# A gated cross-attention block with mixture of experts on one core: the shared expert rebuilt as one unit of 704 columns

## The reference

```python
x = x + tanh(g_xattn[1]) * attention(layernorm(x), ctx)        # 16 heads, the stage before
h = layernorm(x)
probs = softmax(h @ router_w.T)                                # 8 experts
topk_w, topk_idx = top_k(probs, 2); topk_w = topk_w / sum(topk_w)
moe = sum over the two chosen e of topk_w * (silu(h @ gate_w[e]) * (h @ up_w[e])) @ down_w[e]   # 352 wide
shared = (silu(h @ s_gate_w + s_gate_b) * (h @ s_up_w + s_up_b)) @ s_down_w + s_down_b          # 704 wide
x = x + tanh(g_ffn[1]) * (moe + shared)
```

## Time and profile before

| | us |
|---|---|
| median of 3 runs (1182.26 to 1189.67) | 1182.75 |
| span of the profiled execution, first to last instruction | 1146.9 |
| time of that execution around its span | not given by the page |
| TensorE busy, share of span | 1028.8, 90% |
| VectorE | 747.0, 65% |
| ScalarE | 601.8, 52% |
| GpSimd | 456.0, 40% |

### The profile page before, as it was taken

One profiled execution on the slowest core, in us unless ns is written; L12 is line 12 of the kernel. 1 busy time (PEld: TensorE's weight loads), 2 busy tenths in 40 slices (PEclk: granted clock), 3 DMA queues, 4 the chain that ended last, 5 costly groups with the idle time before them and its releaser, 6 DMA issues. The chain is left out here.

```text
span 1146.9 us, 17729 instructions
## 1 busy us (share of the span) xinstructions
PE 1028.8 (90%) x5438; PEld 475.5 (41%) x5439; DVE 747.0 (65%) x1419; ACT 601.8 (52%) x898; POOL 456.0 (40%) x483
## 2 busy tenths in 40 slices
PE   0466889999789999999999998999998899999996
PEld 0243445555423223323322324455445455555542
DVE  6988988888786776578477547745545344443347
ACT  6897999999346776467467565452211111111110
POOL 1100335544410242243134341000657788889065
PEclk9978899999979999999999999998999899999998
DMA  9322930000534234134211004201678888976588
GB/s 325 114 74 80 342 138 1 2 1 9 133 89 107 80 82 116 62 58 94 66 48 44 12 21 136 76 26 52 243 282 170 200 205 207 206 192 146 153 284 291
DMA packets 174204, 142.39 MB, mean 124 GB/s; under 512 B 121364, under 2 KB 137108, under 8 KB 173624
## 3 DMA queue, kind: packets, MB, share of 16 engines
q1 hardware_dynamic: 163560, 110.40, 34.7%
q0 software_dynamic: 8672, 29.76, 7.9%
q10 hardware_dynamic: 1904, 1.38, 0.6%
HBM read 70.93 MB, written 43.37 MB: 100 GB/s over the span
## 5 line engine op out<-in xcount | busy, mean ns | idle before, releaser
L1432 ACT ACTIVATE prob<-p_col,mask_col,any_key 128x512 f32<-128x512 f32 x256 | 186.2, 781 | 103.2 <-PE p_col L1564 102.3
L1653 DVE CUSTOM_DVE_ANT_0 ajunk<-p_row,mask_row 128x512 bf16<-128x512 f32 x256 | 166.2, 686 | 64.1 <-PE p_row L1513 62.5
L1526 PE MATMUL p_out<-prob,v 128*64 128x512 f32 x512 | 138.1, 618 | 0.1
L1332 POOL TENSOR_TENSOR o<-sum_a,rec 32x512 f32<-32x512 f32 x30 | 39.1, 1304 | 186.1 <-DMA rec<-inv_d 184.0
L1513 PE MATMUL p_row<-ks,early_place 99*128 99x512 f16 x256 | 100.5, 395 | 8.7 <-DVE top L1653 8.0
L1564 PE MATMUL p_col<-early_place,ks 101*128 101x512 f16 x256 | 97.7, 385 | 0.9 <-ACT prob L1432 0.3
L2647 DVE SCALAR_TENSOR_TENSOR shid<-s_up,ssilu 128x352 f32<-128x352 f32 x39 | 20.4, 524 | 99.0 <-PE s_up L2565 98.8
L2513 ACT ACTIVATE ssilu<-s_gate 128x352 f32<-128x352 f32 x39 | 18.1, 463 | 124.0 <-PE s_gate L2565 124.0
L2578 PE MATMUL s_down<-mw,shT 128*128 (+1 forms) x351 | 82.0, 379 | 0.0
L2565 PE MATMUL s_gate<-mw,sxT 128*128 x444 | 74.1, 318 | 6.7 <-DMA sxT<-x_slots 6.7
L2565 PE MATMUL s_up<-mw,sxT 128*128 x444 | 73.5, 316 | 0.0
(11 more groups left out here) (354 smaller groups left out, 2077.3 us busy)
## 6 DMA issues: line engine op xcount, KB each, us to landing
x_slots<-nought SPq DMA_DIRECT2D x3, 3328.0 KB, 18.4
y_slots<-y SPq DMA_DIRECT2D x39, 256.0 KB, 2.2
early_place<-in_ctx SPq DMA_DIRECT2D x8, 1024.0 KB, 6.2
early_place<-halves_d SPq DMA_DIRECT2D x45, 128.0 KB, 2.5
halves_d<-halves SPq DMA_DIRECT2D x18, 256.0 KB, 2.1
mstg<-in_L_ffn_gate_w POOLq DMA_DIRECT2D x6, 704.0 KB, 5.7
mstg<-in_L_ffn_up_w POOLq DMA_DIRECT2D x6, 704.0 KB, 6.0
x<-in_x SPq DMA_DIRECT2D x4, 1024.0 KB, 7.3
```

The source lines that it names most:

```text
L1432: nc.scalar.activation(prob[s % 4][:, c, :], p_col[c][:], ACT.Exp, bias=mask_col[:, b, k:k + 1], scale=any_key[:, b:b + 1]).then_inc(t_exp, 1)
L1526: mm = nc.tensor.matmul(p_out[pr][c * 2 * DH:(c + 1) * 2 * DH, :], v1[b % 2][:, k, g, :], prob[n % 4][:, c, :], start=(k == 0), stop=(k == ...
L1653: nc.vector.tensor_tensor_reduce(junk[:, n % 2, :], p_row[n % 2][:], mask_row[:, blk // HPG, :], 1.0, -3e38, ALU.add, ALU.max, top[blk % 2 ...
```

## The change

The shared expert is one unit of 704 columns: five chunks of 128 rows for gate, five for up, and one chunk that holds the last 64 of both (`CHUNKS` 11). The high half of the last 64 hidden rows lies on partitions 0 to 63 and the low half on 64 to 127, so a down product takes 5 x 3 + 2 = 17 passes per 128 tokens in place of 18. Columns come by DMA transpose on SyncE (`turn`), those of batch 0 in attention's last but one block (`turn_kept`). The router stands after batch 1's second pair of chunks. Down products of batch 1 follow batch 2's pairs, and those of batch 2 are put off to the tail: its hidden halves are stored to `hid_d` and read back. Ten pieces of weights replace the old ones. The held weights for the tail come in two loads, at the tenth and fourteenth pair of tiles. TensorE's pairs for batch 2 and for batch 3 from the third chunk on are unrolled one by one with slices by number. Stores of packed weights are ten in place of four. The buffers `spare`, `lines` and the joined PSUM banks only change places.

```diff
+            def turn_kept():
+
+                for t in range(TPB):
+                    sp.wait_ge(t_kl, t + 1)
+                    early.turn(sp, x0T, keep, t, t_x0)
...
+                if blk == BLOCKS - 2:
+                    turn_kept()
...
+CHUNKS = 2 * (SB - 1) + 1
+CW = CHUNKS * P
+SD0 = KB * CW
+HELD = 2
+HW = 2 * HELD * P
+RW = CW - HW
+assert SD0 + SB * D == 2 * WC and 2 * SLAST == P
+HTS = 2 * SB - 1
+S_PARTS = (("gate", 0, 1), ("up", 0, 1), ("gate", 1, 2), ("up", 1, 2), ("gate", 3, 2), ("up", 3, 2), ("both", SB - 1, 1),
+           ("down", 0, 2), ("down", 2, 2), ("down", 4, 2))
+NSP = len(S_PARTS)
+ORDER = [(u, q) for u in range(EARLY) for q in range(len(W_PARTS))]
+MORE = NSP + len(ORDER) - len(W_PARTS) * (2 + EARLY)
 LATE_B = B - 1
+HELD_B = B - 2
 
 
 def rows(m):
@@ -1848,11 +1867,17 @@
     eng.dma_start(t, src).then_inc(s_w[q % 2], 16)
...
+def down_products(hT, wd):
+
+    out = []
+    for m in range(SB - 1):
+        for hs, hm in ((0, 0), (0, 1), (1, 0)):
+            out.append((hT[hs][m], wd(hm, m, P), P))
+    return out + [(hT[0][SB - 1], wd(0, SB - 1, P), P), (hT[0][SB - 1], wd(1, SB - 1, SLAST), SLAST)]
...
+            def turn(b):
+                sp.wait_ge(m_xl, b)
+                for t in range(TPB):
+                    sp.dma_start_transpose(xT[b][:, :, :, t * P:(t + 1) * P].rearrange("p h k s -> p (h k) s"),
+                                           row_of(TPB * b + t)).then_inc(m_xT[b], 16)
+
...
-
-            def weights(u, q):
-                e = UNITS_IN[u]
-                if u < 2:
-                    c = slice(u * EI, (u + 1) * EI)
-                    src = (a["L1_ffn_s_gate_w"][:, c], a["L1_ffn_s_up_w"][:, c], a["L1_ffn_s_down_w"][c, :])
-                else:
-                    src = [a["L1_ffn_" + t][e] for t in ("gate_w", "up_w", "down_w")]
-                sp.wait_ge(m_wl, ready(u, q) - 2)
-                load_part(sp, stg, m_w, q, *src)
-
-            for u, q in ORDER:
-                weights(u, q)
-            for u in range(2):
-                kept = w[:, (SHARED + u) * 2 * WC:(SHARED + u + 1) * 2 * WC].rearrange("p (h c) -> p h c", h=2)
-                sp.wait_ge(m_wl, ready(u, NQ - 1))
-                sp.dma_start(shared_d[u, :, :, 0:MAIN], kept[:, :, 0:MAIN]).then_inc(m_saved, 16)
-                sp.dma_start(shared_d[u, 0:ELAST, :, MAIN:WC], kept[0:ELAST, :, MAIN:WC]).then_inc(m_saved, 16)
-            sp.wait_ge(m_xT, NT)
+            weights_in(sp, 2)
+            weights_in(sp, 3)
+            turn(1)
+            weights_in(sp, 4)
+            weights_in(sp, 5)
+            weights_in(sp, 6)
+            turn(2)
+            weights_in(sp, 7)
+            turn(3)
+            weights_in(sp, 8)
+            weights_in(sp, 9)
+            sp.wait_ge(m_xT[LATE_B], TURNED)
             for h in range(2):
-                sp.dma_start(late_d[h], xT[:, h, :, LATE_B * S:(LATE_B + 1) * S]).then_inc(m_saved, 16)
-            sp.wait_ge(m_turn, TPB)
+                sp.dma_start(late_d[h], xT[LATE_B][:, h]).then_inc(m_saved, 16)
+            weights_in(sp, NSP)
+            weights_in(sp, NSP + 1)
+            sp.wait_ge(m_wl, NSP)
+            held_d, rest_d, down_d = shared_d
+            gates_kept = (SB - 1 - HELD) * P
+            for h in range(2):
+                first = by_row(h)[:, :, 0:2 * (SB - 1) * P].rearrange("p k (n c) -> p k n c", n=2)[:, :, :, 0:HELD * P]
+                for n in range(2):
+                    sp.dma_start(held_d[h, :, :, n], first[:, :, n]).then_inc(m_saved, 16)
+                sp.dma_start(rest_d[h, :, :, 0:gates_kept], by_row(h)[:, :, HELD * P:(SB - 1) * P]).then_inc(m_saved, 16)
+                sp.dma_start(rest_d[h, :, :, gates_kept:], by_row(h)[:, :, (SB - 1 + HELD) * P:]).then_inc(m_saved, 16)
+                sp.dma_start(down_d[h], wide(h)[:, SD0:]).then_inc(m_saved, 16)
+            for j in range(NSP + 2, NSP + len(ORDER)):
+                weights_in(sp, j)
+            sp.wait_ge(m_hl, SB * GB)
+            for m in range(SB):
+                for h in range(2 if m < SB - 1 else 1):
+                    sp.dma_start(hid_d[:, 2 * m + h, :], hT[HELD_B % 2][h][m]).then_inc(m_saved, 16)
             sp.wait_ge(m_scat, SCATTERED)
             for n in range(2):
                 sp.dma_start_transpose(first_xT[:, n].rearrange("p h k t -> p (h k) t"), x_slots[n * P:(n + 1) * P, :]).then_inc(m_first[n], 16)
-            sp.wait_ge(m_saved, 16 * 6)
+            sp.wait_ge(m_saved, 16 * (2 + 2 * 5 + HTS))
 
         @block.gpsimd
         def _(pool):
@@ -1977,11 +2078,11 @@
                 nc.gpsimd.tensor_tensor(rstd[:], veps[:], neg_half[:], ALU.pow).then_inc(m_rstd, 1)
...
+            high_parts(0, 1, 2, 3)
             act.wait_ge(m_rwt, 1)
             nc.scalar.copy(rwT[0][:], p_rw).then_inc(m_rwh, 1)
-            turned(4)
-            turned(5)
-            high(2)
-            hidden(0, 1, lambda: high_parts(1, 2, 3))
-            for t in range(6, 10):
-                turned(t)
-            high(3)
+            high(1)
+            hidden(0, lambda: high_parts(4, 5), lambda: (high(2), high_part(6)), lambda: high_part(7), lambda: None, lambda: high(3))
             act.wait_ge(m_const, CONSTS)
-            hidden(1, 0, lambda: high_part(2, 0), lambda: high_part(2, 1))
-            for t in range(10, NT):
-                turned(t)
-            act.wait_ge(m_shift, 1)
-            nc.scalar.activation(logit[:], logit[:], ACT.Exp).then_inc(m_exp, 1)
-            hidden(1, 1, lambda: high_part(2, 2), lambda: high_part(2, 3))
-            act.wait_ge(m_xl, B - 1)
-            hidden(2, 0, lambda: high_part(3, 0), lambda: high_part(3, 1))
-            hidden(2, 1, lambda: high_part(3, 2), lambda: high_part(3, 3))
+            hidden(1, lambda: high_part(8), shifted_exp(act, nc, m_shift, m_exp, logit), lambda: high_part(9), lambda: high_part(NSP),
+                   lambda: high_part(NSP + 1))
+            hidden(2, lambda: high_part(NSP + 2), lambda: high_part(NSP + 3), lambda: high_part(NSP + 4), lambda: high_part(NSP + 5),
+                   lambda: high_parts(NSP + 6, NSP + 7))
 
         @block.tensor
         def _(pe):
...
+            def weights_ready(g, i):
+
                 if g == 0:
-                    pe.wait_ge(m_wl, ready(n, NQ - 1))
-                pe.wait_ge(m_hl, EB * (u + 1))
+                    pe.wait_ge(m_wl, (2, 4, 4, 6, 6, 7)[i])
+
+            def pair(g, i):
+                c = SB * g + i
+                q = c % 2 * S
+                weights_ready(g, i)
+                need(pe, m_hid, c - 1)
+                chunk(p_gate[:, q:q + S], lambda hs, k: chunk_of(hs, i if i < SB - 1 else CHUNKS - 1, k), g).then_inc(m_gate, 1)
...
-            turn(14, 15)
+            for i in range(SB):
+                pair(0, i)
+            pe.wait_ge(m_xT[1], TURNED)
+            pair(1, 0)
+            pair(1, 1)
             router()
-            gate_up(1, 1)
-            down(1, 0)
+            pair(1, 2)
+            pair(1, 3)
+            pair(1, 4)
             number_slots()
-            gate_up(2, 0)
-            down(1, 1)
-            gate_up(2, 1)
-            down(2, 0)
-            down(2, 1)
+            pair(1, 5)
+            down(0)
+            looped_pairs(2)
+            pair(2, 5)
+            down(1)
...
+            link(nc.vector.tensor_scalar(bias[:, 1, :], bias[:, 1, :], W_UP, None, ALU.mult))
+            statistics(1)
+            low_parts(0, 1)
+            normalise(1)
+            low_parts(2, 3)
+            ready_router()
+            low_rows(1)
+            hidden(0, lambda: (low_parts(4, 5), statistics(2)), lambda: normalise(2), lambda: (low_rows(2), low_part(6)),
+                   lambda: (statistics(3), low_part(7)), lambda: normalise(3))
             low_rows(3)
-            hidden(1, 0, lambda: low_part(2, 0), lambda: low_part(2, 1))
-            add(0, 1)
-            choose()
-            hidden(1, 1, lambda: low_part(2, 2), lambda: low_part(2, 3))
-            add(1, 0)
-            find_slots()
-            hidden(2, 0, lambda: low_part(3, 0), lambda: low_part(3, 1))
-            add(1, 1)
-            hidden(2, 1, lambda: low_part(3, 2), lambda: low_part(3, 3))
-            add(2, 0)
-            add(2, 1)
-
-
-def stage_tiles(nc, sb, ps, sem, st, a, x, keep, x_slots, y_slots, out_d, w, stg, dest, share, expert_of, m_wh, m_wl,
-                bias, bias_dg, gate_dn, shared_d, late_d, m_first, first_xT):
+            hidden(1, lambda: low_part(8), weigh, lambda: (choose(), low_part(9)), lambda: shares(), find_slots)
+            find_owners()
+            down_bias()
...
-            sp.dma_start(late_w[0][:, :, U0:D0], shared_d[0, :, :, U0:D0]).then_inc(e_lu, 16)
-            sp.dma_start(late_w[1][:, :, G0:D0], shared_d[1, :, :, G0:D0]).then_inc(e_lv, 16)
-            for n, done in enumerate((e_ld0, e_ld1)):
-                sp.dma_start(late_w[n][:, :, D0:MAIN], shared_d[n, :, :, D0:MAIN]).then_inc(done, 16)
```

(82 more changed lines are left out.)

616 lines of the change are left out of this document (336 added, 280 removed).

## The result

The changed kernel takes **1202.0 us** (median of 4 runs, 1197.7 to 1206.6), the kernel before beside it 1182.9; the ratio is 1.0132, 95% interval 1.0077 to 1.0186. Forecast were 1181.5 us and at most 1195. Three further comparisons of the two (e2, e9, e14) gave 1.0112, 1.013 and 1.0071 (intervals within 1.004 to 1.021). So the change costs 9 to 19 us by the medians, where I had it at a gain of 1.4.

The account below looks back on a forecast made before the run. TensorE was taken to bound the kernel nearly everywhere. The terms +2.2 - 4.0 - 5.5 + 5.9 gave -1.4 us on a span of 1146.9, plus 35.9 carried over: 1181.5 us, no change, range 1162 to 1195.

Parts of the forecast that it names:

- attention's end: Before the shared stage: four transposes on SyncE delay the chain of sums and reciprocals, so the stage starts 2.2 us later.
- shared stage: Shared expert's stage: about 32 us less TensorE work, mostly lost to waits in batch 0's feeding chain, leaving -4.0 us.
- tile loop: Loop over tiles: moving held-weight loads later shortens one slow transpose of a tile's columns, -5.5 us.
- tail: After the tiles: 52 more products, partly hidden, make TensorE end after the last gather, +5.9 us, bounds 3 and 9.
- no load of a tile's columns over 7 us: Sign in the new trace, tile loop: the slow transpose of 10.94 us would take 5 to 6.
- the three gaps: Batch 0 of the shared stage: TensorE idle about 10, 10 and 6 us, waiting for normalised rows and weight pieces.
- the scatter is hidden: Shared stage: 32 scatter issues at 1.27 us end near T+153 (T the stage's start), before the tiles at T+164.2.
- Unrolling costs nothing, since TensorE's queue runs ahead of the array: TensorE's unrolled products: an added wait and no-op per pair would cost no time.
- The 35.9 us carried over: Whole kernel: median time 1182.75 us less the profiled span 1146.9, assumed the same after the change.
- (c): Shared stage: rival that scatter, not TensorE, ends the stage, so TensorE's new order does nothing; about 1195 us, chance 0.03.
- (b): Rival, slower: transposes and weight pieces delay each other, 5.5 to 8 us; slow tile-loop transpose may stay, +5.5; chance 0.20.
- (a): Shared stage: rival that the feeding chain is shorter, half of 34 us idle goes, 1164.5 us; chance 0.28.

Follow-up runs that it names:

- e2: The changed kernel run again, only TensorE's wait on expert weights clamped at 0: 1198.5 us beside 1188.1 for the kernel before, ratio 1.0112.
- e9: The changed kernel once more, without a limit on indirect DMAs: 1199.4 us beside 1187.9 for the kernel before, ratio 1.013.
- e14: The changed kernel once more, without a limit on indirect DMAs: 1196.3 us beside 1187.3 for the kernel before, ratio 1.0071.
- e17: The changed kernel with ten empty instructions on GpSimd ahead of each indirect DMA, which did not slow it: 1156.0 us beside 1149.2 for the kernel before.
- e1: The kernel before run again for a second profile, only TensorE's wait on expert weights clamped at 0: 1188.3 us beside 1188.1, ratio 1.0002.
- e11: The changed kernel without GpSimd's scaling of staged weight pieces by 256: 1196.7 us.
- e13: The kernel before with at most four indirect DMAs in flight: 1168.2 us beside 1187.3 without the limit, ratio 0.9814.
- e16: The changed kernel with four DMAs in flight, `turn_kept()` behind the block loop, GpSimd's first two weight loads behind its last scatter: 1147.8 us beside 1187.3 before.
- e12: The changed kernel with at most four indirect DMAs in flight: 1157.4 us beside 1187.9 for the kernel before, ratio 0.9776.
- e10: The changed kernel with the third batch's down products back in the shared stage, no copy of hidden lines to memory: 1207.3 us.
- e5 to e8: Four indirect DMAs in flight, kernel before 1163.2 us, changed 1153.8; groups of eight, changed 1163.0, before 1171.7; unaltered kernel before 1147.9.
- e18: The changed kernel with each series of 32 indirect DMAs in four groups of eight: 1163.9 us beside 1149.2 for the kernel before.
- e3: The changed kernel with GpSimd's scatter and gather DMAs held to two in flight: 1189.1 us, one run.

## Why the prediction was wrong, step by step

The terms as forecast and as measured. Without stops: e17 less the execution of the earlier trace rows. With stops: the mean of the four profiles of the changed kernel (1203.0, 1192.9, 1197.9 and 1194.7 us) less e1.

| term | forecast | without stops | with stops |
|---|---|---|---|
| attention's end, to the first shared product | +2.2 | +1.5 | +5.2 |
| shared stage | -4.0 | -6.2 | -1.3 |
| tile loop | -5.5 | +4.1 | +2.3 |
| tail | +5.9 | +7.7 | +7.2 |
| sum | -1.4 | +7.1 | +13.4 |

Single profiles of one kernel differ by 2 to 7 us in a term, so each figure is that rough.

- **The step that failed is the tile loop's -5.5 us**, the largest part of the miss; the loop measured +4.1 us without stops and +2.3 with them. I took the slow transpose of the earlier trace rows (10.94 us, TensorE idle for 6.37) for the work of the held loads of 256-byte pieces just ahead of it, and that with them the idle time would go. It did not: the loop's length less TensorE's busy time is 6.7 and 6.3 us in the two profiles of before, and 7.6 and 9.1 us in those of the changed kernel and of e17. The cause that I named is borne out only in part. In four of the five profiles of the kernel before and its variants a transpose of over 3 us follows these loads, issued 4 to 8 us behind them; in the changed kernel's new places for them it does so in four of fifteen (e11's is the longest). No run left the loads out. What stands in the place of the old idle time has two parts, and I had a term for neither. The first is GpSimd: it needs 181 us from the stage's end on to split the weights of six experts, and TensorE, no longer held up early in the loop, now waits for it; the changed kernel's row:

```profile
1035.15 1.06 PE L2691 MATMUL s_gate<-mw,spare 128*128 x3 [4.42 <-POOL mw L2598]
```

  Such a wait of 2.5 to 4.7 us is in nine of the thirteen profiles of the change with the split and its start unaltered, and none over 2.5 in the five of before, where it may be the early wait that makes TensorE late enough. The second is transposes that are slow at other places: in e13 at 938.79, 967.36, 997.35 and 1027.34 us, so 29 to 30 us apart, which is GpSimd's beat from expert to expert, and in e17 for 6.1 us at 960.06, ahead of any held load. That GpSimd's weight loads do this was not tried. So why the loop keeps its length stays in part open: e16, in which GpSimd starts its split 6 to 11 us sooner against the first tile, has 228.3 us, near the 227.6 that I had forecast, but so has e2 (228.2) with the kernel unaltered and a wait on GpSimd of 2.5 us, and e11 without GpSimd's wait had 235.8. Of the signs that I had named, "no load of a tile's columns over 7 us" failed with this step: the slowest takes 9.4 us in the changed kernel and 12.5 in e17.
- **The shared stage** went about as worked out where nothing stopped (-6.2 against -4.0). Feeding left TensorE the three gaps that I had at some 10, 10 and 6 us, here in the changed kernel's first profile; e17 has 8.65, 7.84 and 5.34:

```profile
728.73 5.26 PE L2201 MATMUL p_gate<-spare,mw 128*128 128x512 f16 x12 [8.70 <-DVE mw L2311]
749.62 5.06 PE L2201 MATMUL p_gate<-spare,mw 128*128 128x512 f16 x12 [7.86 <-DVE mw L2311]
771.48 1.42 PE L2182 MATMUL p_down<-rwT,spare 128*128 128x8 f16 x48 [5.35 <-DMA mw<-mw]
```

  The chunk behind each of the first two runs at half clock and takes 5.26 and 5.06 us instead of 2.75, so some 2.4 us a restart; the 1.8 that I had used for four restarts came from no row. With stops the stage's gain shrinks to 1.3 us, since the stage can't end before GpSimd has issued its last scatter and TensorE has done what is left behind it. That the scatter is hidden, the step on which I spent one sentence, is true of its DMAs and false of its issuing.
- **"Unrolling costs nothing, since TensorE's queue runs ahead of the array"** was not refuted: the late products look like instructions that come late, but they go with at most four indirect DMAs in flight (e12), with the same unrolled code, and the kernel before, with loops, has them too (e1).
- **Attention's end** was mis-sized. The four transposes hold up the reciprocals' rows on the sync engine's queue by their 5.41 us, and TensorE waits 3.2 to 3.6 us for the output, in every profile with them in this place (0.6 to 0.8 before, 0.60 in e16):

```profile
666.24 5.41 SPq L1006 DMA_TRANSPOSE spare<-keep  x4
688.22 0.39 PE L1591 MATMUL p_fill<-wh,oT 128*128 128x512 f16 x1 [3.31 <-POOL oT L1357]
```

  In this profile and in those of e2, e9, e14 and e17 TensorE then works at half pace for some 3 us (8 or 9 products 0.43 us apart instead of 0.22) and needs 7.2 to 7.3 us for what takes 5.6 otherwise.
- **The tail** too: the 52 products cost TensorE 12.8 us (41.1 to 53.9 us busy, against my 12.0), but only some 5 of them are hidden by the last combines, not 6. e10's medians have them better there than in the stage.
- **The 35.9 us carried over** were no constant but the two stops. They come to 38 us before (13.3 in the stage, 24.6 in the tail, e1 against the earlier trace rows) and to some 42 in the changed kernel (18.2 and 24.2, the four profiles against e17), so the sum suffered by some 5 us only; but I had read a kernel that mostly does not run, and the largest loss of both kernels was outside what I looked at. A gap of 3% between span and time was there to be asked about.
- **The rivals.** I gave 0.03 to (c), that the scatter and not TensorE ends the stage, at 1195. Of all it is nearest to what happened, though not by its price: the scatter did not grow, but TensorE stood while it was issued. Of (b) its second half came true, the loop that keeps its 5.5 us; the landings of its first half did not grow (TensorE's gaps are no longer than forecast). (a) is out by the three gaps above. What none had is a cost in both kernels that the profile of before did not show.

**Left open.** Why the other engines stop during GpSimd's series of indirect DMAs; the Trainium skill, "DMA: Bandwidth & Descriptors", section "SWDGE vs HWDGE vs iDMA", says that GpSimd writes their descriptors into rings in SBUF from which all DMA engines read, and no run here shows whether that is the way. Next, why a set of runs has stops or not: the kernel before took 1183 to 1188 us in four sets and 1148 to 1149 in two, and one chip was in both kinds. And whether the stops belong to the kernel at all or to its recording, a rival that no run tested: the seven profiles without stops (before, e5 to e8, e17, e18) have all 1024 landing records of the two series, and the thirteen others all lack some. Those without a limit or with eight in flight have 188 to 247, those with four 596 to 667 (e12, e13, e16) and that with two 931 (e3). Every timed run comes with a span and a clock of its own, so none is known to have gone unrecorded.

## What to carry to other kernels

Where span and timed runs differ by more than a few us, profile the kernel again before costing a change: the profile may hold the one execution without the loss that matters. An engine hidden by another in the profile has a length of its own: compare its chain's end with the one that you shorten, or the gain turns into a wait on it. Long runs of indirect DMAs may want a limit of some four in flight: where nothing stopped it cost the kernel before 1.3% and the changed one nothing that could be told, and where it did stop it gave 1.9% and 3.5%. All of this is for executions with a profile's span; before a wait is put down to "remote" or "issue", see whether the landing records are complete.
